# Class-query scores summed on TensorE, probabilities laid out as (head parity, key), and three filler products in a vision transformer on one core

## The reference

```python
q = x @ Wq + bq;  k = x @ Wk + bk;  v = x @ Wv + bv
attn1 = einsum('bhqd,bhkd->bhqk', rq, rk)
attn2 = einsum('bhqd,qkd->bhqk', rq, rel_k[idx])     # idx: clipped distance of key and query
attn = softmax((attn1 + attn2) / sqrt(128), axis=-1)
w1 = einsum('bhqk,bhkd->bhqd', attn, rv)
w2 = einsum('bhqk,qkd->bhqd', attn, rel_v[idx])
out = (w1 + w2) @ Wo + bo
```

## Time and profile before

| | |
|---|---|
| profiled execution | 279.16 us, span 277.4 us |
| median of the runs | 279.77 us |
| TensorE busy | 246.4 us (89%), weight loads 212.1 us |
| VectorE busy | 166.5 us (60%) |
| ScalarE busy | 135.0 us (49%) |
| GpSimd busy | 60.7 us (22%) |

### The profile page before, as it was taken

How to read it: one execution, slowest core, us unless ns; L and a number is a source line. 1 busy time by engine, 2 the same in 40 slices (tenths; PEclk the granted TensorE clock), 3 DMA queues, 4 the chain that set the end, 5 groups by cost and what they waited for, 6 DMA issues and landing times.

```text
span 277.4 us, 6440 instructions
## 1 busy us (share of the span) xinstructions
PE 246.4 (89%) x2528; PEld 212.1 (76%) x2528; DVE 166.5 (60%) x516; ACT 135.0 (49%) x438; POOL 60.7 (22%) x79
## 2 busy tenths in 40 slices
PE   1999999999877788895599987999999999999993
PEld 1855576898655565675488986999999999999993
DVE  0476888535699999999659745533333333333453
ACT  1543068953387899980003886144434352526200
POOL 8600131297013444365006400000000000000000
PEclk9999999999988999999999999799999999999999
DMA  6940000000000000090000000000000000000005
GB/s 190 308 133 2 1 0 0 2 4 2 0 0 5 1 2 0 16 293 3 5 5 0 0 4 0 2 0 0 2 0 2 0 1 2 0 4 0 0 23 133
DMA packets 6554, 7.95 MB, mean 29 GB/s; under 512 B 833, under 2 KB 5295, under 8 KB 6396
## 3 DMA queue, kind: packets, MB, share of 16 engines
q1 hardware_dynamic: 5260, 6.32, 7.9%
q10 hardware_dynamic: 720, 0.87, 1.2%
q0 software_dynamic: 544, 0.35, 0.5%
HBM read 6.47 MB, written 1.06 MB: 27 GB/s over the span
## 4 chain that ended last, share of the span: by engine, by line
PE 58%; DVE 23%; ACT 7%; issue 4%; POOL 3%; DMA 2%; SPq 1%; DVEq 0%; POOLq 0%
PE banks L995 52%; DVE stb L725 4%; DVE top L741 4%; ACT region_d L514 2%; DMA rows<-in_L_tok_W_sb 2%; DVE xnT L838 2%; PE banks L1198 2%; POOL region_e L319 2%; DVE region_c L766 2%; PE banks L1005 1%; DVE stats L629 1%; DVE stb L644 1%; ACT vbd L451 1%; DVE ntop L748 1%; DVE Sct L706 1%
## 5 line engine op out<-in xcount | busy, mean ns | idle before, releaser
L985 DVE SCALAR_TENSOR_TENSOR KT<-banks,vbd,KT 128x128 f32<-128x128 f32 (+1 forms) x136 | 38.0, 344 | 60.9 <-PE banks L995 60.9
L514 ACT ACTIVATE region_d<-banks,vecs 128x416 f32<-128x416 f32 x80 | 45.5, 611 | 53.7 <-PE banks L995 53.7
L995 PE MATMUL banks<-w_all,region_d 128*128 128x128 f32 (+1 forms) x544 | 64.6, 280 | 0.0
L995 PEld LDWEIGHTS banks<-w_all,region_d 128*128 128x128 f32 (+1 forms) x544 | 62.6, 191 | 1.5 <-ACT region_d L514 0.2
L492 ACT ACTIVATE region_e<-banks,ntop 128x64 f32<-128x64 f32 x128 | 38.3, 330 | 7.2 <-DVE rsum L759 3.9
L995 PE MATMUL banks<-x_hi,w_hi 128*128 128x416 f32 x80 | 29.4, 368 | 0.9 <-ACT region_d L514 0.9
L995 PE MATMUL banks<-x_lo,w_hi 128*128 128x416 f32 x80 | 28.2, 353 | 0.0
L995 PE MATMUL banks<-x_hi,w_lo 128*128 128x416 f32 x80 | 28.2, 352 | 0.0
L492 ACT ACTIVATION_READ_ACCUMULATOR region_e<-banks,ntop 128x1 f32 x128 | 27.8, 217 | 0.0
L347 POOL TENSOR_TENSOR region_e<-region_e,rsum 128x512 f32<-128x512 f32 (+1 forms) x16 | 16.5, 1032 | 35.6 <-DVE rsum L759 35.6
L1198 PE MATMUL banks<-kc,stb 128*128 128x128 f32 x64 | 11.1, 298 | 8.5 <-DVE stb L725 8.5
(11 more groups left out here) (221 smaller groups left out, 395.4 us busy)
## 6 DMA issues: line engine op xcount, KB each, us to landing
region_a<-in_x SPq DMA_DIRECT2D x2, 512.0 KB, 6.5
region_a<-in_x SPq DMA_DIRECT2D x1, 1024.0 KB, 10.7
w_sb<-in_L_ffn_W SPq DMA_DIRECT2D x1, 1024.0 KB, 5.5
out<-KT SPq DMA_DIRECT2D x8, 128.0 KB, 2.4
region_d<-in_L_attn_rel_v SPq DMA_DIRECT2D x2, 260.0 KB, 9.4
kc<-in_consts ACTq DMA_DIRECT2D x1, 336.0 KB, 5.3
region_d<-in_L_tok_eps_in ACTq DMA_DIRECT2D x2, 128.0 KB, 7.0
region_d<-in_L_tok_W_w ACTq DMA_DIRECT2D x1, 128.0 KB, 7.6
```

Of the source, the lines that this page charges most:

```text
L514: a.activation(HB[:, e % 2, s, blk * FB:(blk + 1) * FB], bank[h_bank(i)][:, 0:FB], ACT.Gelu, bias=vecs[:, v:v + 1]).then_inc(S["gelu_ok"], 1)
L985: last = v.scalar_tensor_tensor(acc[0:m, t, :], bank[out_bank(u)][0:m, i * C:(i + 1) * C], comb[0:m, t, e:e + 1], acc[0:m, t, :], op0=ALU. ...
L995: return t_.matmul(o, l, r, start=start, stop=stop)
```

## The change

- *Values.* `xnTd` and its ScalarE copy go. `values_of` multiplies `xnT` directly: four products per block, one bank per block. `evac_v` copies the two halves of partitions to the two halves of `VBD`, unscaled; the other quarters stay zero, cleared once by GpSimd (`memset` of `vbd`, 4096 columns, after the `mhalf` one). The partition order of `VBD`, `RVBD`, the probabilities and `PT` becomes (parity, key).
- *Class-query scores.* GpSimd's additions to `KT`, ScalarE's scalings of `KT`, `turn_cls(4..7)`, four reductions and the turn of `Sct` go. ScalarE writes two small operands from a 0/1 pattern scaled by the class query (`q0w`, `q0r`, in the former buffer of the embedding weights); 16 products with a window of `q0w` that slides by 8 columns, and one with `q0r` and the relative-position vectors, add up in bank 7.
- *Fillers.* `keep_warm(3, spare=4)` ahead of the relative-position products.

```diff
-    k[:, K_KP:K_KP + 2] = p % 2 == np.arange(2)
+    k[:, K_KP:K_KP + 2] = p // NPATCH == np.arange(2)
...
+        q0w = wnT[:, 0:248]
+        q0r = wnT[:, 256:384]
...
-                sp_.dma_start(region_d[par:P:2, 3072:3072 + QC * HD], src).then_inc(S["d_rvd"], 16)
+                sp_.dma_start(region_d[NPATCH * par:NPATCH * par + NPATCH, 3072:3072 + QC * HD], src).then_inc(S["d_rvd"], 16)
...
             link(g.memset(mhalf[:, :], -0.5))
+            g.memset(vbd[:, :], 0.0).then_inc(S["vz_ok"], 1)
...
                     pool.wait_ge(S["KM_ok"], 4)
+                    pool.wait_ge(S["in_ps"], 4)
+                    g.memset(q0w, 0.0).then_inc(S["q0z_ok"], 1)
...
-            for n in range(NBLK):
-                b = slice(n * BLK, (n + 1) * BLK)
-                pool.wait_ge(S["KM_ok"], n + 1)
-                kt = KT[:, b].rearrange("p (b q) -> p b q", q=NPATCH)
-                g.tensor_tensor(kt, kt, relkT[:, 65:129].unsqueeze(1).to_broadcast(bb), ALU.add)\
-                    .then_inc(S["ua_ok"], 1)
...
-                ev = e_[:, 0:P * js].rearrange("p (j k s) -> p j k s", j=js, s=2)
-                rv = r_[:, 0:2 * js].rearrange("p (j s) -> p j s", j=js).unsqueeze(2).to_broadcast([P, js, NPATCH, 2])
+                ev = e_[:, 0:P * js].rearrange("p (j s k) -> p j s k", j=js, s=2)
+                rv = r_[:, 0:2 * js].rearrange("p (j s) -> p j s", j=js).unsqueeze(3).to_broadcast([P, js, 2, NPATCH])
...
-                a.activation(xnTd[:, b, :], bank[2 + n % 2][:, :].unsqueeze(2).to_broadcast([P, BLK, 2]),
-                             ACT.Copy).then_inc(S["xnTd_ok"], 1)
...
-                for half in range(2):
-                    u = 2 * n + half
-                    act.wait_ge(S["v_ps"], u + 1)
+                act.wait_ge(S["v_ps"], n + 1)
+                if n == 0:
+                    act.wait_ge(S["vz_ok"], 1)
+                for b2 in range(2):
                     for s in range(2):
                         last = a.activation(
-                            VBD[:, 4 * u:4 * u + 4, :].rearrange("p b (j s d) -> p (b j) s d", s=2, d=HD)[:, :, s],
-                            bank[half][:, :].rearrange("p (m s d) -> p m s d", s=2, d=HD)[:, :, s],
-                            ACT.Copy, scale=kc[:, K_KP + s:K_KP + s + 1])
-                    last.then_inc(S["VBD_ok"], 1)
+                            VBD[NPATCH * s:NPATCH * (s + 1), 8 * n + b2:8 * n + 8:2, :]
+                            .rearrange("p r (j s d) -> p r j s d", s=2, d=HD)[:, :, :, s],
+                            bank[n % 2][NPATCH * b2:NPATCH * (b2 + 1), :]
+                            .rearrange("p (r j s d) -> p r j s d", r=4, s=2, d=HD)[:, :, :, s], ACT.Copy)
+                last.then_inc(S["VBD_ok"], 1)
...
-                if i % 2 == 1:
-                    n = i // 2
-                    b = slice(n * BLK, (n + 1) * BLK)
-                    act.wait_ge(S["ua_ok"], n + 1)
-                    a.activation(KT[:, b], KT[:, b], ACT.Copy, scale=clsv[:, 0:1]).then_inc(S["uc_ok"], 1)
+                if i == 1:
+                    act.wait_ge(S["q0z_ok"], 1)
+                    a.activation(q0w[:, 120:128], kc[:, K_E8:K_E8 + H], ACT.Copy, scale=clsv[:, 0:1])\
+                        .then_inc(S["q0_ok"], 1)
+                    a.activation(q0r, kc[:, K_E8:K_E8 + P], ACT.Copy, scale=clsv[:, 0:1]).then_inc(S["q0_ok"], 1)
...
-                if p < 2:
-                    red(4 + 2 * p)
-                    red(5 + 2 * p)
                 if p == 2:
                     class_scores()
...
-                pe.wait_ge(S["xnTd_ok"], n + 1)
+                pe.wait_ge(S["xnT_ok"], n + 1)
                 if n == 0:
                     pe.wait_ge(S["xi_ok"], 4)
-                for half in range(2):
-                    if n:
-                        pe.wait_ge(S["VBD_ok"], 2 * n - 1 + half)
-                    for i in range(4):
-                        im = 8 * n + 4 * half + i
-                        last = mm(bank[half][:, i * C:(i + 1) * C],
-                                  xnTd[:, im * NPATCH:(im + 1) * NPATCH, :].rearrange("p t s -> p (t s)"), wv)
-                    last.then_inc(S["v_ps"], 1)
+                if n >= 2:
+                    pe.wait_ge(S["VBD_ok"], n - 1)
+                for i in range(TPB):
+                    t = n * TPB + i
+                    last = mm(bank[n % 2][:, i * C:(i + 1) * C], xnT[:, t * P:(t + 1) * P], wv)
+                last.then_inc(S["v_ps"], 1)
...
+            pe.wait_ge(S["h0_ok"], 3)
+            keep_warm(3, spare=4)
             pe.wait_ge(S["QP_ok"], 4)
-            pe.wait_ge(S["xnTd_ok"], 4)
+            pe.wait_ge(S["xnT_ok"], 4)
...
+            def class_products(pairs):
+
+                for r in pairs:
+                    if r == 0:
+                        pe.wait_ge(S["q0_ok"], 2)
+                        pe.wait_ge(S["tc_red"], 4)
+                    mm(bank[7][:, 0:P], q0w[:, 120 - H * r:248 - H * r], KT[:, r * P:(r + 1) * P], r == 0, False)
...
-                if p < 2:
-                    turn_cls(4 + 2 * p)
-                    turn_cls(5 + 2 * p)
+                if p < 3:
+                    class_products(range(6 * p, min(6 * p + 6, PAIRS)))
                 if p == 2:
-
-                    pe.wait_ge(S["tc_red"], 8)
-                    t_.transpose(bank[7][:, 0:P], Sct[:, :], ident)
+                    mm(bank[7][:, 0:P], q0r, relkT[:, 65:129].unsqueeze(1).to_broadcast([P, 2, NPATCH]), False, True)
                     mm(bank[7][:, P:P + 1], kc[:, K_E8:K_E8 + P], clsv[:, 4:5]).then_inc(S["c0_ps"], 1)
```

More of the change, by code:

```diff
@@ L160, in vit_kernel @@
         Sc = sb("Sc", PAIRS * H)
-        Sct = sb("Sct", PAIRS * H)
         cx = sb("cx", 2 * QC)
@@ L199, in vit_kernel @@
         d_cls d_w3 xperm_ok xT_ps xT_evA xT_evD g_ps gate_ok  in_ps xi_ok y_ps h0_ok ve_ok
[L200 to L201 removed]
+        rstd_ok xn_ok xnT_ps xnT_ok vz_ok q_ps k_ps v_ps QT_ok KT_ok QP_ok KM_ok VBD_ok cls_ps clsv_ok a2_ps
+        a2_evA a2_evD kcq_ok tc_ok q0z_ok q0_ok tcT_ps tc_red c0_ps cx_ok cexp_ok p0d_ok p0T_ps ptc_ok pc_m ve_c
         rstd_c s1_ps st_ok s_ps top_ok dc_ok e_ok r_ok half_ok pn_ok pc_ok pt_ps pt_ok w1_ps w1_ev rep_ok pcT_ps pcx_ok
@@ L489, in _ @@
                 src = bank[2 + p % 2][:, :].rearrange("p (j k s) -> p j s k", j=PJ, s=2)
-                dst = SP[p % 4][:, 0:512].rearrange("p (j k s) -> p j s k", j=PJ, s=2)
+                dst = SP[p % 4][:, 0:512].rearrange("p (j s k) -> p j s k", j=PJ, s=2)
                 for h in range(H):
@@ L785, in class_probs @@
                 link(v.reciprocal(sml[:, 8:10], r2))
-                v.tensor_tensor(p0d[:, :].rearrange("p (b k s) -> p b k s", b=2, s=2),
-                                cv[:, :, 0:NPATCH].unsqueeze(3).to_broadcast([P, 2, NPATCH, 2]),
-                                sml[:, 8:10].unsqueeze(2).unsqueeze(3).to_broadcast([P, 2, NPATCH, 2]), ALU.mult)
+                v.tensor_tensor(p0d[:, :].rearrange("p (b s k) -> p b s k", b=2, s=2),
+                                cv[:, :, 0:NPATCH].unsqueeze(2).to_broadcast([P, 2, 2, NPATCH]),
+                                sml[:, 8:10].unsqueeze(2).unsqueeze(3).to_broadcast([P, 2, 2, NPATCH]), ALU.mult)
                 link(v.tensor_tensor(sml[:, 10:12], cv[:, :, NPATCH], sml[:, 8:10], ALU.mult))
@@ L846, in _ @@
                     js = PJ // 2
-                    ev = SP[(PAIRS - 1) % 4][:, P * js:512].rearrange("p (j k s) -> p j k s", j=js, s=2)
+                    ev = SP[(PAIRS - 1) % 4][:, P * js:512].rearrange("p (j s k) -> p j s k", j=js, s=2)
                     rv = rsum[:, 8 * ((PAIRS - 1) % 2) + 2 * js:8 * ((PAIRS - 1) % 2) + 8]\
-                        .rearrange("p (j s) -> p j s", j=js).unsqueeze(2).to_broadcast([P, js, NPATCH, 2])
+                        .rearrange("p (j s) -> p j s", j=js).unsqueeze(3).to_broadcast([P, js, 2, NPATCH])
                     v.tensor_tensor(ev, ev, rv, ALU.mult).then_inc(S["half_ok"], 1)
@@ L1086, in turn1 @@
                 if n >= 2:
-                    pe.wait_ge(S["xnTd_ok"], n - 1)
+                    pe.wait_ge(S["xnT_ok"], n - 1)
                 for i in range(TPB):
@@ L1140, in _, with turn_cls @@
             values_of(3)
-            def turn_cls(g):
-                n = g % 4
-                src = tc_ if g < 4 else KT
-                pe.wait_ge(S["tc_ok" if g < 4 else "uc_ok"], n + 1)
-                if g >= 4:
-                    pe.wait_ge(S["tc_red"], g - 3)
+            def turn_cls(n):
+                pe.wait_ge(S["tc_ok"], n + 1)
                 for i in range(TPB):
                     t = n * TPB + i
-                    last = t_.transpose(bank[4 + n][:, i * P:(i + 1) * P], src[:, t * P:(t + 1) * P], ident)
+                    last = t_.transpose(bank[4 + n][:, i * P:(i + 1) * P], tc_[:, t * P:(t + 1) * P], ident)
                 last.then_inc(S["tcT_ps"], 1)
+            pe.wait_ge(S["h0_ok"], 3)
+            keep_warm(3, spare=4)
             pe.wait_ge(S["QP_ok"], 4)
```

(8 more changed lines are left out.)

6 lines of the change are left out of this document (1 added, 5 removed).

## The result

The kernel after took 276.61 us, the one before 278.99 (medians of twelve runs each): ratio 0.991, interval 0.9885 to 0.9935. The forecast was 278.0 from a level of 279.77. Of the 1.39 us between forecast and result, 0.78 is that level (the longer series puts the kernel before at 278.99), and 0.61 is the gain: 2.38 us where the forecast had 1.77 (279.77 less 278.0; its sum is 1.76).

A forecast was written before the change was run, and what follows sets the result against it. It took TensorE (89% busy), in places alternating with ScalarE, as the bound before the pair loop and VectorE within it. Gains 0.85 + 0.46 + 0.45 = 1.76 us took the 279.77 median to 278.0, own range 277.2 to 278.6.

The forecast's parts named there:

- Projection stretch: Ahead of the relative-position products: less value work starts them at 52.47 instead of 53.32, gain 0.85 us, ends 0 and 1.2.
- The stall: Before the fifth relative-position group: without GpSimd's KT additions, ScalarE's copy is in time, gain 0.46 us, ends 0 and 0.5.
- Class scores in the loop: First three pair turns: VectorE's savings mostly taken back by TensorE; 2.4 GHz there gains 0.45 us, ends -0.5 and +0.9.
- Layout: Probabilities stored as (parity, key): same counts and columns, zero gain; up to 0.4 us either way.
- The clear: GpSimd's 4096-column clear of the value buffer takes 4.2 us, over at 15.5, before the copies at 16.02; costs 0.
- "The same instructions, shifted": From 92.83 us on, loop, end of attention and expert stage are the same in both kernels, taken as merely shifted.
- (a): TensorE's clock falls to 1.2 GHz for 3 us within the relative-position products, losing some 1.5 us: 279.5; chance 0.13.
- (b): A slow clear shuts out VectorE's permuting copies at 16.02, costing 4.8 or 3.5 us: 282.8 or 281.5; chance 0.13.
- (c): The clear also shuts out VectorE's two-operand instructions; next weight step waits until 15.5, +2.5 us: 280.5; chance 0.07.
- (d): More gain: half-speed stretch near 174 us does not return, or products vanish behind VectorE: 276.4; chance 0.07.
- (e): The first stretch is not shortened (slow 64-partition copies, or query copy bound elsewhere): 0.9 left, 278.9; chance 0.10.

The follow-up runs named there:

- values_filled: Kernel before with only the values and layout part, plus five identity products in the stall ahead of the fifth relative-position group: 277.81 us, ratio 0.9972.
- after_clear_twice: Whole change with GpSimd's clear of the value buffer done twice: 278.08 us in a single execution.
- class_only: Kernel before with the class-query part alone, values as before, no fillers: 277.47 us, ratio 0.9938.
- before_warm_pos24: Kernel before plus nine identity products ahead of the experts, without the five identity products of pair turn 16: 280.33 us, ratio 0.9974.
- values_only: Kernel before with the values and layout part alone, no fillers, class-query work as before: 286.34 us, ratio 1.0258.
- after_warm_no_fillers: Whole change plus nine identity products ahead of the experts, without its three fillers: 274.31 us, ratio 0.9830, leaving out one run of 290.02 us.
- after_warm_experts: Whole change plus nine identity products in TensorE's pauses ahead of the experts: 273.65 us, ratio 0.9806.
- after_warm_pad5: Whole change plus nine identity products ahead of the experts and five in pair turns 8 to 12: 274.61 us, ratio 0.9854.

## Why the prediction was right in sign and small in size

The mechanism of the main terms held, and what failed are sizes. The result lies 1.39 us under the forecast and 0.59 under the low end of its own range (277.2). Of the 1.39, 0.78 is the level of the kernel before, which the forecast took from three runs; as a ratio the forecast was 0.994, with a range of 0.991 to 0.996, and 0.991 came out. The other 0.61 are three terms of the sum that were too small: the projection stretch by 0.21, the stall by 0.26, the class scores by 0.14 on average. The step that failed most clearly is the stall, whose stated ends (0 and 0.5) leave the measured 0.72 out.

- *Projection stretch: 0.85 forecast, 1.06 measured.* The mechanism held in each step: last turn held by VectorE, TensorE the later of the two behind it. The terms were rounded up from grouped rows: 0.98 for the values of a block, where the step is 0.89, and 1.84 for queries and keys, where it is 1.78. These make 0.20 us over the four pieces. The bound of 1.2 without fillers was wrong: without them the start was at 18.90 too, not 0.35 earlier, since VectorE's masked queries end at 52.09 of a start at 52.15.
- *The stall: 0.46 forecast, 0.72 measured.* The cause of the stall and its end were right. What was wrong is to read its price off its idle time, 0.47 us; the distance from group to group, 2.49 us over the stall against 1.79, was in the trace of the kernel before.
- *Class scores in the loop: 0.45 forecast; 0.24 with the clock undisturbed on both sides, 0.92 in the two profiled ones.* The working had all but nothing left at 2.4 GHz and gave the 0.45 to the dip at 81. In truth the dip stands in four of the five traces with the old class turns and the old values (14.48 to 14.99; 14.31 without it). Up to the fifth maximum it is in none of the ten with the class part whose clock had not fallen earlier (14.06 or 14.07); it is missing in values_filled too (14.30), so it is not a fixed property of the old turns. The five have a mean of 14.66, so the average gain is 0.59: 0.24 of work and 0.35 of clock. One of the ten, after_clear_twice, has 1.2 GHz from 86.6 to 93.4, just behind its fifth maximum, and takes 30.67 us from there to the 16th instead of 29.96: the dip can also move, as the forecast's low end had it. class_only, which has only this part, is without a dip in the loop; that it is the filled idle time that does it was argued ahead and not tested by itself.
- *Layout: 0, and 0 it was.* The exponentials, GpSimd's scaling (mean 1032 ns) and the turns kept their times, and from the 5th to the 16th maximum both kernels take 29.95 us.
- *The clear: 4.2 us and nothing on the path forecast, 3.52 and nothing measured.* Half of the scaling's pace for an operation that reads nothing was a fair estimate. The margin to the copies was 0.68 us.
- *Sum:* 1.06 + 0.72 + 0.59 = 2.37 against 1.76; 2.38 is the difference of the medians. That the two agree so closely is luck: by the interval of the ratio the gain is 1.8 to 3.2 us, and the sum leaves out the last stage, whose 1.5 us may belong to the change.
- *"The same instructions, shifted":* true of the instructions, and wrong for the times of any pair of executions. The stage before the residual scatters by 2 us, the half clock ahead of the experts lasted 3.4 or 6.8 us, and the first token turn came at 32.7 to 34.1, once at 36.6. Whether it holds for the mean is open.
- *Rivals.* (a) didn't happen to the whole change, but its mechanism was the strongest force in this case: it costs the values part alone 8.5 us (286.34 against 277.81 with the stall filled, in another series; 8.0 by the ratios). The forecast looked for it at the wrong place: behind the pause of 1.20 us ahead of the last turn the clock stayed at 2.4 GHz up to the relative-position products in every trace. (b) did not happen at 0.86 ns a column; its mechanism did with the clear over at 18.36. From where on it costs was not measured; the margin was 0.68 us. (c) did not happen. (d) had the half clock near 174 gone; it stayed, and the nine products there are worth another 2.5 to 3.9 us. (e) did not happen.

What stays open: whether the gap's place is worth some 0.7 us, whether the change makes the half clock ahead of the experts longer, why one pause lets the clock fall in one run and not in the next, and what the rest of the +4.2 us in before_warm_pos24 is.

The best version here is the whole change with the nine products ahead of the experts: 273.4 to 274.1 us in three series, ratios 0.9820, 0.9806 and 0.9769.

## What to carry to other kernels

Two edits can be worth more together than apart because one takes away a wait that the other makes longer: price each edit with the others undone, and look for what gets late when only one engine gets faster. Read a stall's price from the steps between equal instructions on both sides of it, not from its idle time. Before pricing saved work by TensorE, look at the pauses that it leaves just ahead of a long run of products, and try to fill those. Here nine identity products cost 0.15 us in one stage and took 2.3 to 3.9 us off the whole, and five in the stall of values_only took 8.5 off; three ahead of the relative-position products changed nothing in the median. And don't read a gain of 1 or 2 us from one pair of traces: two executions of one kernel differed by as much in a single stage.

## What the runs showed of the hardware that was not expected

- After its clock had fallen, TensorE stayed at 1.2 GHz from 61 to 85 us (values_only) and from 55 to 89 (after_warm_no_fillers), though its records on the relative-position products (64 rows, 64 columns) show it busy for 3.00 of 3 us, from 63 to 78 and from 54 to 81. The same products kept 2.4 GHz in every other trace. Pauses of 1.14 and 0.60 us came ahead of the two falls.
- In two other traces the clock fell, for 3.4 us, with no pause over 0.15 us in the 8 us before (after_warm_experts at 159.6, after_warm_pad5 at 158.0).
- Nine identity products in two pauses of about 1 us took 2.3 to 3.9 us off, though TensorE's next turn waits there for ScalarE with or without them.
- In the relative-value stage, where 128 records take 2.15 us, TensorE stopped by itself at places 128 records with their weight loads apart, for up to 1.9 us, and at some of these places in some executions for less than 0.15.
- A GpSimd clear runs at 0.86 ns a column (3.52 us for 4096) and held VectorE's two permuting copies (SBUF to SBUF) until it ended, 3.07 us instead of 1.29, while a copy from PSUM beside such a clear kept 0.69.
